# Attention ordered by batch with rows divided on GpSimd, and experts in two passes over the tokens

## What is computed

```python
# layer 0, attention: energy = (ctx Wq + bq)(ctx Wk + bk)^T; x_m = xn @ softmax(energy)^T
# layer 0, feed-forward: two linear layers on quantised activations and weights
y = bit_linear(x, gate_w, gate_norm_w)
gate, up = jnp.split(y, 2, axis=-1)
h = gate * jax.nn.sigmoid(gate) * up
out = bit_linear(h, down_w, down_norm_w)
# layer 1, cross attention, 16 heads of 128
q = rmsnorm((hidden_states @ Wq).reshape(B, Sq, H, D), gq)
k = rmsnorm((encoder_hidden_states @ Wk).reshape(B, Skv, H, D), gk)
v = (encoder_hidden_states @ Wv).reshape(B, Skv, H, D)
attn = jax.nn.softmax(jnp.einsum('bqhd,bkhd->bhqk', q, k) * scale, axis=-1)
out = jnp.einsum('bhqk,bkhd->bqhd', attn, v).reshape(B, Sq, H * D) @ Wo
# layer 1, feed-forward: 64 experts of width 64, the best 8 of each token, and one shared expert
logits = x @ gate_w.T
topv, topi = jax.lax.top_k(logits, TOP_K)
rw = jax.nn.softmax(topv, axis=-1)
```

## Time and profile before

| | us |
|---|---|
| median of 3 runs | 694.0 (691.27 to 697.71) |
| span of the profiled execution | 690.4 |
| TensorE busy | 629.1 (91%) |
| VectorE busy | 506.5 (73%) |
| ScalarE busy | 409.9 (59%) |
| GpSimd busy | 135.5 (20%) |

### The profile page before, as it was taken

The page is one execution under the profiler, slowest core; times in us unless marked ns, Lnnn a source line. Parts: engine busy times, 40 slices in busy tenths (PEclk is TensorE's granted clock), DMA queues, the critical chain, the costliest instruction groups (busy, mean ns, idle before and its releaser), DMA issues.

```text
span 690.4 us, 12148 instructions
## 1 busy us (share of the span) xinstructions
PE 629.1 (91%) x3664; PEld 535.7 (78%) x3664; DVE 506.5 (73%) x1214; ACT 409.9 (59%) x1053; POOL 135.5 (20%) x107
## 2 busy tenths in 40 slices
PE   5825687999999999999997798999999999999997
PEld 3612476999999999999986686888888888888884
DVE  3799985888888888888887774655666566666654
ACT  4648767988888889888883253333333333333333
POOL 2027352343424333343331100000000000000000
PEclk9869899999999999999998799999999999999998
DMA  8200010000000000100000003344444443334311
GB/s 293 98 23 0 1 47 0 25 25 24 24 25 24 24 23 23 28 18 0 1 0 24 23 1 100 106 114 116 113 112 116 112 115 107 106 106 106 106 30 61
DMA packets 14575, 41.43 MB, mean 60 GB/s; under 512 B 2448, under 2 KB 3088, under 8 KB 14416
## 3 DMA queue, kind: packets, MB, share of 16 engines
q1 hardware_dynamic: 14544, 41.07, 20.3%
HBM read 39.75 MB, written 1.31 MB: 59 GB/s over the span
## 4 chain that ended last, share of the span: by engine, by line
PE 77%; DVE 9%; ACT 3%; issue 1%; POOL 0%; DVEq 0%; ACTq 0%
PE bank L250 23%; PE bank L252 22%; PE bank L251 22%; PE bank L595 3%; PE bank L574 2%; PE bank L565 2%; DVE u L1197 1%; PE bank L623 1%; DVE x L1433 1%; ACT bank L983 1%; PE bank L523 1%; DVE stats L1186 1%; DVE rowmax L1404 1%; DVE m_lo L1442 1%; ACT att L1006 0%
## 5 line engine op out<-in xcount | busy, mean ns | idle before, releaser
L1114 ACT ACTIVATE inter_hi<-inter 128x512 fp32r<-128x512 f32 (+1 forms) x66 | 41.7, 632 | 143.8 <-DVE inter L1582 138.3
L250 PE MATMUL bank<-xnT_hi,e_hi 128*128 128x512 f32 x256 | 102.8, 402 | 0.1
L252 PE MATMUL bank<-xnT_hi,e_lo 128*128 128x512 f32 x256 | 102.3, 399 | 0.0
L251 PE MATMUL bank<-xnT_lo,e_hi 128*128 128x512 f32 x256 | 102.2, 399 | 0.0
L1565 DVE TENSOR_TENSOR prod<-gate_s,bank 128x512 f32<-128x512 f32 (+1 forms) x66 | 45.4, 687 | 60.5 <-PE bank L252 60.5
L363 POOL TENSOR_TENSOR rqk<-msq,minus_half 128x8 f32<-128x8 f32 x32 | 52.4, 1637 | 164.8 <-DVE msq L1398 164.7
L1587 DVE TENSOR_TENSOR inter_lo<-inter,inter_hi 128x512 fp32r<-128x512 f32 (+1 forms) x66 | 45.7, 692 | 44.8 <-ACT inter_hi L1114 44.7
L1006 ACT ACTIVATE att<-bank,shift,rqk 128x256 f32<-128x256 f32 x128 | 71.2, 570 | 3.3 <-DVE shift L1411 3.3
L1433 DVE SCALAR_TENSOR_TENSOR x<-bank,rowinv,x 128x256 f32<-128x256 f32 x128 | 55.8, 477 | 7.6 <-PE bank L252 7.5
L250 PEld LDWEIGHTS bank<-xnT_hi,e_hi 128*128 128x128 f32 x256 | 49.2, 192 | 11.6 <-ACT gate_s L1108 0.5
L251 PEld LDWEIGHTS bank<-xnT_lo,e_hi 128*128 128x128 f32 x256 | 49.0, 191 | 11.7
(11 more groups left out here) (235 smaller groups left out, 1719.6 us busy)
## 6 DMA issues: line engine op xcount, KB each, us to landing
w_all<-w_rows SPq DMA_DIRECT2D x60, 256.0 KB, 3.9
e_raw<-in_expert_w SPq DMA_DIRECT2D x32, 384.0 KB, 4.1
wqk_raw<-in_head_qk SPq DMA_DIRECT2D x8, 384.0 KB, 3.1
wvo_raw<-in_head_vo SPq DMA_DIRECT2D x8, 384.0 KB, 3.0
gate_raw<-in_gate_wT SPq DMA_DIRECT2D x1, 1408.0 KB, 11.2
x<-in_x_tok SPq DMA_DIRECT2D x2, 512.0 KB, 6.1
outT<-final SPq DMA_DIRECT2D x4, 256.0 KB, 2.1
down_raw<-in_down_wT SPq DMA_DIRECT2D x1, 640.0 KB, 12.3
```

What stands on the lines that cost most here:

```text
L250: pe.matmul(out, l_hi, r_hi_, start=start, stop=False, skip_group_check=True)
L251: pe.matmul(out, l_hi, r_lo_, start=False, stop=False, skip_group_check=True)
L252: return pe.matmul(out, l_lo, r_hi_, start=False, stop=stop, skip_group_check=True)
L1114: act.activation(inter_hi[0:rows, slot, :], inter[0:rows, slot, :], ACT.Copy).then_inc(a_Ihi, 1)
```

## The change

- Attention goes batch by batch: group g is batch g // 8, head pair g % 8, and the loops are unrolled over the 32 groups. The split weights of all 8 pairs (`w_hi`, `w_lo`) and all m stay in SBUF from the first batch on.
- Softmax's rows are divided before they are transposed, by GpSimd, 128x512 per head (`normalise_att`). So the outputs of all 16 heads accumulate in one bank, and VectorE adds them to x once per batch. GpSimd's power is split into one for k and one for q, of 4 columns each.
- Tokens 0-511 are complete after group 15. Their statistics, normalisation, router and weights are worked out inside groups 16 to 26.
- The experts go over tokens 0-511 for all 32 pairs, with the routing of tokens 512-1023 inside steps 2 to 11, and then over 512-1023 for all pairs, with the shared expert behind each pass. So `e_raw` is loaded and split 64 times instead of 32. The buffers of the split weights are 4 instead of 3, and the spreads are of 512 tokens instead of 1024. Token weights are no longer spread by matmul for the first steps.
- In the start, two head pairs are loaded ahead of `gate_raw`, `ctxT_lo` moves behind attention A and `ctx_lo` from the place between the down scales to that behind the gate rounding, four head pairs are split (`split_w`, `low_w`), and `proj_k` of two groups and `turn_rows` of batch 0 stand inside the down loop.

The diff, cut to its core. GpSimd:

```diff
+            def normalise_att(n, h):
+
+                pool.wait_ge(v_inv, n * 2 + h + 1)
+                a = att[:, n % 2, h, :, :]
+                pool.tensor_tensor(a, a, rowinv[:, n % 2, h, :].unsqueeze(2).broadcast_to([P, 2, SEQ]),
+                                   ALU.mult).then_inc(g_att, 1)
...
+            rms_k(0)
+            low_w(EARLY)
+            power(5, vare[:, 2:8], rstd[:, 2:8], 6)
+            rms_k(1)
...
+            for g in range(GROUPS):
+                n = g + 4
+                if n - 1 < GROUPS:
+                    rms_k(n - 1)
+                if g + 1 < GROUPS:
+                    for h in range(2):
+                        normalise_att(g + 1, h)
+                if n - 1 < GROUPS:
+                    rms_q(n - 1)
+                if g + EARLY + 1 < PAIRS:
+                    low_w(g + EARLY + 1)
```

TensorE:

```diff
+            def turn(g, h):
+                pe.wait_ge(g_att, g * 2 + h + 1)
+                wait(pe, v_Tlo, g * 2 - 1 + h)
...
+                    mm = split_mm(pe, bank4(YBK)[:, t, :], o_hi[:, h, c], o_lo[:, h, c],
+                                  m_hi[:, p, h, :], m_lo[:, p, h, :], p == 0 and h == 0 and t == 0,
+                                  p == PAIRS - 1 and h == 1)
...
+                if g in (19, 20):
+                    turn_rows(2, g - 19, KBK)
+                if g == 21:
+                    router(0, KBK)
+                if g == 25:
+                    turn_weights(0, KBK)
+                if g == 26:
+                    turn_shared(0, KBK)
...
+            for q in range(2, 12):
+                step(q % 4, q % 2, 0, q, q)
+                experts_down((q - 1) % 4, (q - 1) % 2, 0, q - 1)
+                if q in (3, 4):
+                    pe.wait_ge(v_Tlo, 2 * GROUPS)
+                    turn_rows(2, q - 1, TBK[q - 3])
+                if q == 6:
+                    router(1, 2)
```

VectorE:

```diff
-                    dve.scalar_tensor_tensor(xb, bank4(YBK)[:, t, :], rowinv[:, b, t, h:h + 1], xb, ALU.mult,
-                                             ALU.add).then_inc(v_Y, 1)
+                dve.wait_ge(t_Y, 16 * b + 16)
+                xb = x[:, 2 * b:2 * b + 2, :]
+                dve.tensor_tensor(xb, bank4(YBK), xb, ALU.add).then_inc(v_Y, 1)
...
+                if g + 1 < GROUPS:
+                    for h in range(2):
+                        row_inverse(g + 1, h)
+                if g % PAIRS == 0 and g:
+                    add_output(g // PAIRS - 1)
+                if g == 17:
+                    dve.wait_ge(v_Y, 2)
+                    tile_stats(0, 4)
+                    ask_rstd(0, 4)
+                if g == 18:
+                    ask_pow()
+                    normalise(0, 4)
+                if g == 21:
+                    choose(0)
+                if g == 24:
+                    weights(0)
...
+            def step(r, slot, s, expert, turn):
+                times_up(slot, s)
+                times_loaded(slot, s, r % 2, turn)
+                low_inter(slot, s)
+                dve.wait_ge(a_Ehi, expert + 1)
+                dve.tensor_tensor(e_lo[:, (r + 2) % 4, :], e_raw[:, r % 2, :], f(e_hi[:, (r + 2) % 4, :]),
+                                  ALU.subtract).then_inc(v_Elo, 1)
...
+            for q in range(2, 12):
+                step(q, q % 2, q, q + 2, q // 2)
+                if q == 2:
+                    tile_stats(4, TILES)
+                    ask_rstd(4, TILES)
+                    ask_pow()
+                    normalise(4, TILES)
```

ScalarE and SP:

```diff
+            def step(r, slot, s, q, expert_turn):
+                silu(slot, s)
+                act.wait_ge(t_D, q - 1)
+                high_inter(slot, s)
+                act.wait_ge(l_exp[r % 2], expert_turn * 16 + 16)
+                act.activation(e_hi[:, (r + 2) % 4, :], e_raw[:, r % 2, :], ACT.Copy).then_inc(a_Ehi, 1)
...
+            def first_half(q, par):
+                sp.wait_ge(v_Elo, q - 3)
+                load_expert(par, q)
+                sp.wait_ge(v_mul2, q - 1)
+                spread_rows(par, q, 0)
...
+            def second_half(e, par):
+                sp.wait_ge(v_Elo, e + (EPAIRS - 3))
+                load_expert(par, e)
+                sp.wait_ge(v_mul2, e + EPAIRS)
+                spread_rows(par, e, 1)
```

More of the change, by code:

```diff
@@ L687, in _, with router @@
-            turn_k(1, 1, 1)
-            pe.wait_ge(a_sqQ, 12)
-            pe.wait_ge(a_rawK, 3)
-            scores(0, 0)
-            pe.wait_ge(a_sqQ, 16)
-            pe.wait_ge(a_rawK, 4)
-            pe.wait_ge(g_ctx, 2)
-            pair(0, 0, first=True)
-            with pe.Fori(1, PAIRS // 2) as i:
-                pair(i * 2 - 1, 1)
-                pair(i * 2, 0)
-            pair(PAIRS - 1, 1, last=True)
-            def router(half):
+            def router(half, bk):
                 pe.wait_ge(g_rw, 1)
@@ L823, in _ @@
[L823 to L825 removed]
+            turn_q2(0)
+            for i in range(TILES):
+                if i + 1 < TILES:
+                    turn_q2(i + 1)
+                down(i)
+                if i == 4:
+                    pe.wait_ge(g_ctx, 1)
+                    proj_k(0, 0, True)
+                if i == 5:
+                    proj_k(1, 1, True)
+                if i == 6:
+                    turn_rows(1, 0, 2)
@@ new lines, in keep_shared, with split_e, silu @@
+            def keep_shared(half, bk):
+                act.wait_ge(t_wk, half * 2 + 2)
+                act.activation(shT[:, half * 512:half * 512 + 512], bank[bk][0:2, :], ACT.Copy).then_inc(a_wk, 1)
+            def split_e(q):
+                act.wait_ge(l_exp[q % 2], (q // 2) * 16 + 16)
+                act.activation(e_hi[:, q % 4, :], e_raw[:, q % 2, :], ACT.Copy).then_inc(a_Ehi, 1)
+            def silu(slot, s, rows=P):
+                act.wait_ge(t_G, s + 1)
+                wait(act, v_mul1, s - 1)
+                act.activation(gate_s[0:rows, slot, :], bank[GB][0:rows, :], ACT.Silu).then_inc(a_silu, 1)
@@ new lines, in last_steps, with finish @@
+            def last_steps(r, slot, s, turn):
+                times_up(slot, s)
+                times_loaded(slot, s, r % 2, turn)
+                low_inter(slot, s)
+            def finish(t):
+                for hb in range(2):
+                    dve.wait_ge(t_F, 2 * t + hb + 1)
+                    dve.scalar_tensor_tensor(final[:, hb, t, :], bank[ACC[hb][t]][:, :], tg[:, 3:4],
+                                             xT_end[:, hb, t * 512:(t + 1) * 512], ALU.mult, ALU.add).then_inc(v_out, 1)
@@ L1647 @@
+            for r in range(4):
+                q = 2 * EPAIRS - 4 + r
+                if r < 2:
+                    step(r, (r + 1) % 2, q + 1, q + 2, q // 2)
+                else:
+                    last_steps(r, (r + 1) % 2, q + 1, q // 2)
+            times_up(1, 2 * EPAIRS + 1, EI)
+            times_shared(1, 2 * EPAIRS + 1, 1)
+            low_inter(1, 2 * EPAIRS + 1, EI)
+            finish(1)
 def kernel(**inputs):
```

1478 lines of the change are left out of this document (720 added, 758 removed).

## The result

The changed kernel takes 699.0 us in the median (694.8 to 701.8, 18 runs) where the kernel before takes 692.0 (689.4 to 697.7, 18 runs): ratio 1.0088, interval 1.0067 to 1.0108. So the changed kernel is 0.9% slower, which the interval tells from no change, and 2 us above the forecast of 697. The profiled execution has a span of 696.9 against 690.4.

A forecast was written before the change was run, and what follows sets the result against it. TensorE's matmul issue was taken to bound groups and expert steps, with waits between them. Stretches of 114.5 + 250.3 + 34.9 + 280.3 + 13.5 made a 693.5 us span; with the median 3.6 above the span, 697, range 684 to 713.

The forecast's parts named there:

- Division on GpSimd: In each attention group: two divisions at 1.04 us each, slack 0.3 us before TensorE wants the second, nothing lost.
- Rival 2: Attention groups: GpSimd's chain binds each group; at 1.4 us per division 11 us more, 708 us; chance 0.11.
- Start: From 0 to the group loop's first query transposes at 114.1: +0.4 us, good to 2 either way.
- Groups: Groups 0 to 27: 235.6 + 14.7 us, from TensorE's routing 5.2, one-off VectorE work with bank waits 8.1, `shift` 1.4.
- full hold: One-off VectorE work in groups 18, 21, 24: held up by GpSimd's divisions; with no hold, 3 us instead of 8.1.
- Group 28 to step 2: From group 28 to step 2's silu: 34.9 us, TensorE's work 29.3, waits 3.1 and 2.5 for e_lo(2); gain 30.6.
- Steps: Expert steps 2 to 63: 254.9 us (61 at 4.18) plus 25.4 for routing, shared expert, stalls, clock and SyncE's queue.
- L: Landing time of a pair's expert load: taken as 3.2 us, with up to 3.38 fitting in two steps.
- circle: Expert steps: product, spreads, load, split and next products take 4.98 + L us, to fit in two steps, 8.36.
- term of 1.0: Expert steps in SP's loops: 1.0 us added for stray long loads.
- Rival 1: Expert steps: loads bind, at a landing of 4.1 us or more; 710 us, 725 at 4.7; chance 0.17.
- Rival 3: Groups and steps: one-off work is hidden, taking back 14.5 us, about 683 us; chance 0.25.

The follow-up runs named there:

- gpsimd_plus: The changed kernel with one more GpSimd instruction per group, a power of 128x4 between the scaling of k_raw and the two divisions; ratio 1.0152 to the kernel before.
- sync_straight: The changed kernel with SyncE's loop over pairs 18 to 31 of the first pass written out straight; ratio 1.0062 to the kernel before.
- exact_count: The changed kernel with the second pass's spreads of pairs 0 and 1 waiting for one second product fewer; 694.0 us, ratio 1.0025 to the kernel before.
- second_routing_out: load_first with the routing of tokens 512-1023 left out of steps 2 to 11; ratio 0.9824 to the kernel before.
- load_first: The changed kernel with SyncE issuing the load of pair q+1 ahead of the spread of pair q, in both passes; 692.2 us, ratio 1.0007 to the kernel before.

## Why the prediction was right, and where its terms were off

The forecast held in its main statement: a gain of some 33 us between attention and experts and at the end, given back by one-off stalls and moved work. Its terms, one by one:

- **Division on GpSimd.** Right in price (1.05 on average against 1.04) and in effect (plain groups unchanged). The room was 0.7 instead of 0.3 by gpsimd_plus. Rival 2 did not happen, and at 1.4 us a division it would have cost next to nothing, its 0.7 being just the room.
- **Start: 0.4 forecast, 1.0 measured.** The terms that the forecast names don't add up to 0.4 (-1.4, -2.1 and 1.8 are -1.7, and the rest isn't given as one sum). TensorE's two waits for k there are 1.27 and 1.14 us, not 2.8 each.
- **Groups: 14.7 forecast, 8.8 measured.** TensorE's routing is 4.6, 0.6 less than put. The failed step is that of the one-offs: 8.1 and 1.4 for `shift`. The group lengths, less 8.13 and TensorE's work, give 0.6 for stats, 2.1 for u (against 2.0), 1.0 for choose (2.1) and 1.2 for weights (2.7), the rest nothing: 4.9. With the 4.6 that is 9.5, and the loop's other groups are 0.7 shorter in sum than before. The full hold was right for u only. In choose and weights it met one instruction each (0.92 and 1.07 us instead of 0.43), and the small ones ran beside GpSimd at their usual length. `shift` took its usual 0.15 in these groups, so nothing of the 1.4.
- **Group 28 to step 2: 34.9 forecast, 39.5 measured.** The wait for e_lo(2) is the forecast's 2.5 to the digit, but the clock that fell behind it, 1.2, wasn't priced there; it fell in four executions of eight. Other waits are 4.4 (1.24, 0.33, 1.56, 0.87 and 0.35 by the timeline) against 3.1. The rest is TensorE's own work, put too low: it is busy 31.3 us in this stretch in sync_straight and exact_count, at full clock, against 29.3. Which of its terms is short I haven't worked out.
- **Steps: 25.4 added by forecast, 29.7 measured.** Routing with its stalls and clock was put at 14.7 and is 12.0. The shared expert, turn_x and `finish` were put at 7.0; second_routing_out, less 1.9 for the write-out and 61 steps at 4.20, leaves 7.1. The step itself is 4.20, not 4.18, which makes 1.2. SyncE's queue was put at 2.7 and is 2.6 for the weights, 1.9 for the output and 3.6 for the wait that counts one product too many (2.2 to 2.6 in the other kernels of this order). The last is the step that failed: I took `e + EPAIRS` for the second pass's form of the first pass's wait and didn't count it out for pairs 0 and 1. With the 254.9 of the steps and 0.3 of the loads these make 283.6 of the 284.6.
- **Loads.** L was 3.5 instead of 3.2. The circle's terms as the forecast lists them add up to 4.93, not 4.98, so its limit is L = 3.43, and 59.04 us over 14 intervals is 4.93 + L for L = 3.50, as measured. The term of 1.0, for both loops, is of about the right size: in the first, 59.04 is 0.3 more than load_first takes, and 0.5 to 1.3 more than the four other kernels with spreads first.
- **Rival 1** (the circle of loads binds) happened in a mild form: the circle reached its limit and hardly passed it. What it did was take the room from the loads, so that other waits in the queue reached TensorE. It fits the changed kernel's stretch being long: four other kernels with the same queue order took 280.2 to 281.4, the forecast's 280.3 among them. In three of these the loads landed at a median of 3.2 to 3.4 us between 473 and 545 us, instead of 3.5; in sync_straight at 3.6, but issued earlier, as said above. Why they landed later in one kernel than in another isn't shown. The rival's upper figure, 725 at L = 4.7, doesn't follow from its own sum, which gives about 723.
- **Rival 3** (one-off work hidden) took back 5 us of the groups' terms, and the groups gave back 5.9, yet not by its mechanism alone, since u was held. In the steps 2.7 of its 7 came, and the wait at step 2 stood in full.

The Trainium skill's advice on elementwise work with two inputs on GpSimd (GPSIMD Engine Reference, section Engine selection), about twice VectorE's time, would give 1.39 us a division as an estimate; measured are 1.05 on GpSimd and 0.69 alone on VectorE, a factor of 1.5. The exclusive lock on a shared port pair of which the Trainium skill speaks (SBUF — State Buffer, section SBUF: two separate sides) fits the 3.37 and the 1.34 us. It fits too that VectorE gets in between two GpSimd instructions, since that section gives the pair away "for the whole instruction".

Open remain what decides whether the clock falls behind a wait of 2.50 us, and why loads land at a median of 3.0 us with loads first and 3.4 to 3.5 with spreads first; that the spreads' bytes go ahead of them was not tested by itself.

## What to carry to other kernels

When a transfer's circle just fits its period, don't ask what the circle costs but what else stands in its queue: at nearly no room a write-out or a count that is one too high reaches the bound engine, by 2 us and more each here, and reordering two issues can win more than mending them one by one. Find the gap inside an engine's cycle before placing one-off work: pieces of up to 0.76 us cost nothing in the middle of VectorE's step, and behind it all that goes beyond 0.4 us. A wait of 2.5 us on TensorE cost 2.1 in some executions and 3.3 in others, where the granted clock fell behind it, so read the clock in more than one trace before you price a wait. And compare a stretch with several kernels that share its code: held against the changed kernel alone, load_first's gain in the steps looked about twice as large.

## What the runs showed of the hardware that I hadn't expected

- VectorE, held by GpSimd, gets its turn once per GpSimd instruction: three u in a row end 0.14 us behind a scaling and two divisions of 1.04 to 1.09. Not everything is held: rowmax, which reads PSUM, keeps its 0.69 while a division runs (211.49 in the changed kernel), and so do the four statistics, which read SBUF, with 1.39 (266.84).
- The same wait of 2.50 us on TensorE was followed by a granted clock of 0.57 to 0.65 over 4 us in four kernels' executions and by 1.00 in four others.
- An elementwise product of 128x512 by a broadcast column costs GpSimd 1.05 us and, alone, VectorE 0.69; where it stood made no difference to the whole (1.0088 against 1.0075).
- A 384 KB load landed in 3.0 us (2.8 to 3.6) when issued ahead of its spreads (load_first) and in 3.5 (3.1 to 4.4) behind 256 KB of them (changed kernel), both between 473 and 545 us.
